# A scan kernel with experts: B as two float32r parts, and new lists of work

## What is computed

```python
delta = softplus(x @ Wd + bd)
Bm = x @ WB + bB                       # 16 values per token
Cm = x @ WC + bC
A = -exp(A_log)
def step(h, inps):
    x_t, d_t, B_t, C_t = inps
    bar_A = exp(minimum(d_t[:, :, None] * A, 2.0))
    bar_B = clip(d_t[:, :, None] * B_t[:, None, :], -2.0, 2.0)
    h = clip(bar_A * h + bar_B * x_t[:, :, None], -100.0, 100.0)
    return h, sum(h * C_t[:, None, :], -1) + x_t * D_param
routing = softmax(flat @ Wr + br)      # top 1 of 4 experts
hid = silu(flat @ up_w[e] + up_b[e])
out = ssm_out + top1_w * (hid @ down_w[e] + down_b[e])
x = layernorm(x + layernorm(out) * ln_w + ln_b)
x = layernorm(x + (silu(x @ wg.T) * (x @ wu.T)) @ wd.T)
```

## Time and profile before

| | us |
|---|---|
| runs: median of 3 (lowest, highest) | 859.77 (859.2, 875.19) |
| the profiled execution: its time | 854.52 |
| the profiled execution: its span | 852.7 |
| busy: DVE, PE, POOL, ACT | 706.2, 652.5, 558.3, 517.1 |
| a steady batch | 92.7 |
| after the last scan | 138.4 |

### The profile page before, as it was taken

One profiled execution on the slowest core, in us unless ns is written; L12 is line 12 of the kernel. 1 busy time (PEld: TensorE's weight loads), 2 busy tenths in 40 slices (PEclk: granted clock), 3 DMA queues, 4 the chain that ended last, 5 costly groups with the idle time before them and its releaser, 6 DMA issues.

```text
span 852.7 us, 14265 instructions
## 1 busy us (share of the span) xinstructions
PE 652.5 (77%) x4267; PEld 529.3 (62%) x4322; DVE 706.2 (83%) x1458; ACT 517.1 (61%) x970; POOL 558.3 (65%) x452
## 2 busy tenths in 40 slices
PE   3366567876789768995889778986988668889686
PEld 1144345864588547874688557964787447778555
DVE  3699999889999999799999999999979999324452
ACT  5274084777577946775777847784678413575534
POOL 1257458658875887578865886588766886525442
PEclk9587696997799959996799869995999859799988
DMA  3333346785467637674578536764667465375410
GB/s 110 123 127 121 127 146 208 244 265 163 146 221 241 204 118 229 201 214 169 171 236 249 177 120 223 237 210 154 209 190 228 140 198 185 107 219 181 132 37 26
DMA packets 82088, 149.32 MB, mean 175 GB/s; under 512 B 9404, under 2 KB 51144, under 8 KB 81992
## 3 DMA queue, kind: packets, MB, share of 16 engines
q1 hardware_dynamic: 69192, 135.13, 49.7%
q0 software_dynamic: 4096, 8.40, 3.1%
q10 hardware_dynamic: 8704, 4.72, 1.9%
HBM read 132.80 MB, written 15.40 MB: 174 GB/s over the span
## 4 chain that ended last, share of the span: by engine, by line
PE 32%; DVE 30%; issue 13%; POOL 12%; ACT 6%; DMA 5%; DVEq 1%; SPq 1%; another core or an unknown queue 0%; POOLq 0%; ACTq 0%
DVE state L1304 8%; DVE state L1318 7%; PE psU L767 6%; POOL prod L1350 5%; PE psT L781 5%; PE psY L637 4%; DVE psB L1299 4%; PE psD L661 3%; POOL rows_in L1371 3%; DMA xT_sb<-in_xT 2%; DMA weights<-in_w_pack 2%; DVE attn L1271 2%; PE psU L808 2%; PE psB L631 2%; PE psU L810 2%
## 5 line engine op out<-in xcount | busy, mean ns | idle before, releaser
L1350 POOL TENSOR_TENSOR prod<-state,c_wide 128x1024 f32<-128x1024 f32 x128 | 302.0, 2367 | 129.7 <-DVE state L1318 109.1
L1299 DVE TENSOR_TENSOR psB<-dx,psB 128x512 f32<-128x512 f32 x256 | 166.7, 684 | 19.3 <-PE psB L631 9.6
L631 PE MATMUL psB<-parts,sel 128*128 128x512 bf16 x202 | 94.0, 470 | 109.7 <-DVE state L1318 65.0
L893 ACT ACTIVATE decay<-delta,a_sb 128x1024 f32<-128x1024 f32 x128 | 141.4, 1141 | 50.1 <-DVE state L1318 48.8
L637 PE MATMUL psY<-ident,prod 128*128 128x128 f32 x1024 | 169.5, 323 | 2.6 <-DVE state L1318 1.5
L1318 DVE TENSOR_TENSOR_SCAN state<-decay,state,psB 128x512 f32<-128x512 f32 x128 | 163.3, 1276 | 8.7
L637 PEld LDWEIGHTS psY<-ident,prod 128*128 128x128 f32 x1024 | 152.0, 170 | 11.6 <-issue 7.9
L1304 DVE TENSOR_TENSOR_SCAN state<-decay,psB 128x512 f32<-128x512 f32 x128 | 155.2, 1213 | 0.1
L934 ACT ACTIVATE hid<-psU,weights 128x128 f32<-128x128 f32 x352 | 100.2, 370 | 50.1 <-PE psU L767 48.4
L631 PEld LDWEIGHTS psB<-parts,sel 128*128 128x128 bf16 x256 | 26.3, 103 | 160.7 <-DVE state L1318 92.7
L767 PE MATMUL psU<-yT_sorted,weights 128*128 128x128 f32 x704 | 95.8, 280 | 10.1 <-DMA weights<-in_w_pack 4.1
(11 more groups left out here) (163 smaller groups left out, 1030.0 us busy)
## 6 DMA issues: line engine op xcount, KB each, us to landing
c_wide<-c_rows SPq DMA_DIRECT2D x128, 512.0 KB, 5.0
weights<-in_w_pack SPq DMA_DIRECT2D x88, 514.0 KB, 4.0
xT_sb<-in_xT SPq DMA_DIRECT2D x8, 512.0 KB, 4.6
y_sorted<-rows_in SPq DMA_DIRECT2D x16, 256.0 KB, 3.3
xt<-in_x SPq DMA_DIRECT2D x8, 512.0 KB, 5.6
rows_out<-result SPq DMA_DIRECT2D x16, 256.0 KB, 5.3
out<-x ACTq DMA_DIRECT2D x16, 256.0 KB, 2.9
y_sorted<-rows_in SPq DMA_DIRECT2D x8, 192.0 KB, 4.8
```

Source lines behind the costliest of these rows:

```text
L631: pe.matmul(tokens(psB, c, h), sel[:, s, :], parts[:, c.n % 2, h * HALF:h * HALF + c.hw], start=True, stop=True).then_inc(b_ready, 1)
L893: nc.scalar.activation(decay[:, g % NDECAY, w], delta[:, n % 2, w], ACT.Exp, scale=a_sb[:, s:s + 1]).then_inc(decay_ready, 1)
L1299: v.tensor_tensor(tokens(psB, c, h), dx[:, n % 2, h * HALF:h * HALF + c.hw], tokens(psB, c, h), ALU.mult).then_inc(inp_ready, 1)
L1350: g_.tensor_tensor(prod[:, g % NPROD, w], state[:, g % NSTATE, w], c_wide[:, g % NC, w], ALU.mult).then_inc(prod_ready, 1)
```

## The change

B is cut in two float32r parts. `parts` and `sel` become float32r tiles; the matmul writes B and C to partitions 0 to 31 and 64 to 95 alone; ACT's second copy (`bc_mid`) works on 32 partitions and raises `parts_ready` itself; the DVE task `bc_low` goes, and so does the semaphore `parts_mid`. `sel` keeps one column per state, which the matmul reads 128 times. Beside that all the lists are new: the steady ones and those for the last batches. Line numbers behind L1123 fall by 4.

```diff
--- before.py
+++ after.py
 DVE_ORDER = [
...
-    (-2, "scan_rest", 10), (-1, "bc_low"), (-4, "affine", 1), (-4, "stats", 1, 1), (-4, "aggr", 1, 1),
+    (-2, "scan", 10), (-2, "scan_rest", 10), (-4, "centre", 1), (-4, "affine", 1), (-4, "stats", 1, 1),
...
@@ -365,7 +366,7 @@
         minus_ident = sb("minus_ident", [128, 128], F32R)
         ident127 = sb("ident127", [128, 128])
         selcol = sb("selcol", [128, S])
-        sel = sb("sel", [128, S, 128], BF16)
+        sel = sb("sel", [128, S], F32R)
         aux_sb = sb("aux_sb", [128, 129 + L // ROWS + MAX_BLOCKS])
         bias3 = sb("bias3", [96, D], BF16)
         of_block = sb("of_block", [96, 2, MAX_BLOCKS], BF16)
@@ -381,7 +382,7 @@
         zb = sb("zb", [D, L])
         sp = sb("sp", [D, L])
         bcf = sb("bcf", [128, L])
-        parts = sb("parts", [128, 2, L], BF16)
+        parts = sb("parts", [128, 2, L], F32R)
         bmax = sb("bmax", [128, 2 * NJ], BF16)
         delta = sb("delta", [D, 2, L])
         dx = sb("dx", [D, 2, L])
@@ -460,7 +461,6 @@
 
         parts_high = sem("parts_high")
         rest_ready = sem("rest_ready")
-        parts_mid = sem("parts_mid")
         parts_ready = sem("parts_ready")
         c_stored = sem("c_stored")
         softplus_steps = sem("softplus_steps")
@@ -628,7 +628,7 @@
                     pe.wait_ge(parts_ready, c.n + 1)
                     if c.n == 0:
                         pe.wait_ge(setup_dve, SETUP)
-                pe.matmul(tokens(psB, c, h), sel[:, s, :], parts[:, c.n % 2, h * HALF:h * HALF + c.hw],
+                pe.matmul(tokens(psB, c, h), sel[:, s:s + 1].to_broadcast([128, 128]), parts[:, c.n % 2, h * HALF:h * HALF + c.hw],
                           start=True, stop=True).then_inc(b_ready, 1)
 
             def add_turned(c, term, src, first, last, done):
@@ -668,7 +668,7 @@
                 pe.wait_ge(state_ready, S * (c.n + 1))
                 pe.wait_ge(gathered[0], 16 * NJ * (c.with_half[0] + 1))
                 for k in range(WARM):
-                    pe.matmul(psB[:, 0:HALF], sel[:, 0, :], parts[:, c.n % 2, 0:HALF], start=True, stop=True)
+                    pe.matmul(psB[:, 0:HALF], sel[:, 0:1].to_broadcast([128, 128]), parts[:, c.n % 2, 0:HALF], start=True, stop=True)
 
             def fill(b, c, task):
 
@@ -865,7 +865,7 @@
                     act.dma_start(c_rows[n % 2, :, w], bcf[S:2 * S, w]).then_inc(c_stored, 16)
                 if name == "bc_mid":
                     act.wait_ge(rest_ready, n + 1)
-                    nc.scalar.activation(parts[64:128, n % 2, w], rest[64:128, w], ACT.Copy).then_inc(parts_mid, 1)
+                    nc.scalar.activation(parts[64:96, n % 2, w], rest[64:96, w], ACT.Copy).then_inc(parts_ready, 1)
                 if name == "softplus":
                     exp_table()
                     wait(act, flag_steps, 2 * n - 1)
@@ -1028,7 +1028,7 @@
             v.memset(peak[:, :], 0.0).then_inc(consts_ready, 1)
             dve.wait_ge(consts_ready, 2)
             v.memset(first_block[:, 0:1], 0.0).then_inc(consts_ready, 1)
-            setup(v.tensor_copy(sel[:, :, :], selcol[:, :].rearrange("p (s o) -> p s o", o=1).to_broadcast([128, S, 128])))
+            setup(v.tensor_copy(sel[:, :], selcol[:, :]))
             setup(v.tensor_scalar(minus_ident[:, :], ident[:, :], -1.0, None, ALU.mult))
             setup(v.tensor_scalar(ident127[:, :], ident[:, :], 127.0, None, ALU.mult))
             dve.wait_ge(ff_in, 48)
@@ -1118,10 +1118,6 @@
                     dve.wait_ge(delta_ready, n + 1)
                     v.tensor_tensor(dx[:, n % 2, w], delta[:, n % 2, w], xT_sb[:, n % 2, w], ALU.mult
                                     ).then_inc(dx_ready, 1)
-                if name == "bc_low":
-                    dve.wait_ge(parts_mid, n + 1)
-                    v.tensor_tensor(parts[96:128, n % 2, w], rest[96:128, w], parts[96:128, n % 2, w], ALU.subtract
-                                    ).then_inc(parts_ready, 1)
                 if name == "bound":
                     (h,) = args
                     dve.wait_ge(delta_ready, n + 1)
@@ -1353,7 +1349,7 @@
                     pool.wait_ge(parts_high, n + 1)
 
                     wait(pool, flag_steps, 2 * n - 1)
-                    g_.tensor_tensor(rest[:, w], bcf[:, w], parts[:, n % 2, w], ALU.subtract).then_inc(rest_ready, 1)
+                    g_.tensor_tensor(rest[:, w], bcf[:, w], parts[:, n % 2, w].bitcast(F32), ALU.subtract).then_inc(rest_ready, 1)
                 if name == "bound_input":
                     pool.wait_ge(x_abs_ready, n + 1)
                     pool.wait_ge(dinv_ready, n + 1)
@@ -1425,7 +1421,7 @@
     pad = np.zeros(32, wb.dtype)
     bcb = np.concatenate([a["attn_bB"], a["attn_bC"]])
     sel = np.zeros((128, S), np.float32)
-    for row in (0, 64, 96):
+    for row in (0, 64):
         sel[row:row + S] = np.eye(S, dtype=np.float32)
     up_w, down_w = a["attn_up_w"], a["attn_down_w"]
     w_pack = np.concatenate([
@@ -1441,8 +1437,8 @@
     arrays = {
         "xT": x.transpose(0, 2, 1), "x": x, "a_log": a["attn_A_log"], "d_param": a["attn_D_param"].reshape(D, 1),
         "wd": a["attn_Wd"], "bd": a["attn_bd"].reshape(D, 1),
-        "wbc": np.concatenate([wb, wc, none, wb, wc, wb, wc], axis=1),
-        "bbc": np.concatenate([bcb, pad, bcb, bcb]).reshape(128, 1),
+        "wbc": np.concatenate([wb, wc, none, wb, wc, none], axis=1),
+        "bbc": np.concatenate([bcb, pad, bcb, pad]).reshape(128, 1),
         "wr": a["attn_Wr"], "br": a["attn_br"].reshape(1, E), "w_pack": w_pack,
         "biases": a["attn_down_b"], "aux": aux,
         "ln_w": a["attn_ln_w"].reshape(1, D),
```

262 lines of the change are left out of this document (133 added, 129 removed), and 3 rows, old and new, of the table SP_ORDER.

## The result

The changed kernel takes 880.0 us (median of 4 runs, 875.1 to 884.7), the kernel before 860.9 (median of 4, 859.2 to 875.2): ratio 1.022, 95% interval 1.016 to 1.028. It is slower by 2.2%, where 848 us and a small gain were forecast. The profiled execution took 877.7 us (span 875.9) against 854.5, at the same mean clock (0.851 of full speed in both).

The account below looks back on a forecast made before the run. No engine bounds alone; in steady batches DVE nearly does (88.0 of 92.7 us), PE next. First batch -1.0, two batches -2.5, five at -1.8 -9.0, tail +0.3: -12.2 us, 842.3 profiled, 848 as median, range 839 to 858.

Parts of the forecast that it names:

- the replay of `centre` 1 and `affine` 1 behind `scan_rest` 10: DVE, steady batch in new order: `centre` 1 stalls 1.12 us behind POOL's product 9, then all eight operations need 2.25 us.
- the 2.10 us stall: DVE's `affine` 1, slowed by POOL's L1361 (3.24 us against 1.14): claimed to go in five batches, -2.10 us each.
- -0.21 + 1.12 for `centre` 1: DVE, per steady batch: -0.21 us as `centre` 1 no longer waits for L1356, +1.12 us waiting behind product 9.
- the stall stays: Rival, chance 0.33: L1361 gets in front of one of the eight operations, DVE waits 2.1 us again; 855 us.
- The rival "Slower": Chance 0.08, 867 us: POOL comes first everywhere, so DVE's `centre` 1, `affine` 1 and `dx` wait 1.12, 2.10 and 2.36 us.
- its further part: Chance 0.02, 900 us: float32r matmul with one column read 128 times is slower than L808, +6.4 us a batch.
- The first batch's -1.0 us: First batch: dropped `bc_low` saves 1.3 us on the path, POOL's 4-byte subtraction costs 0.24; net about -1.0 us.
- the -2.5 us for the two steps without an `affine` 1: Two batches whose `bc_low` (76.7 and 152.9 us) has no `affine` 1 near: -1.26 us each, -2.5 in all.
- The float32r price: PE's spread matmuls: weight load 190 to 192 ns against 98, throughput unchanged; handovers +0.3 us per batch, tail +0.3.
- four direct places per batch: Handovers where `scan` s+1 directly follows `scan_rest` s (15-0, 1-2, 6-7, 11-12), eight before: each pays 0.1 us more at high clock.
- the dropped step's own time: DVE's `bc_low` (L1123), one instruction per batch, 8 in all: removing it frees 1.26 us each with the issue behind it.
- The steady batch of 90.5 to 91 us: Sign that the forecast is right: steady batch at 90.5 to 91 us, from 92.7, -1.8 us taken per batch.

Follow-up runs that it names:

- the mended one: The change with `centre` 1 back ahead of `scan_rest` 9, `combine` 0 ahead of `scan_rest` 3 (10 in last list), last list's first `combine` 1 ahead of `scan_rest` 15: 854.8 us.

## Why the prediction was wrong

**The step that failed** is the replay of `centre` 1 and `affine` 1 behind `scan_rest` 10: "So `centre` 1 stalls 1.12 us, until 427.07", then "With each piece at its length it ends at 429.3 to 429.5" for L868, and from both "So the 2.10 us stall goes". I replayed the batch with durations of another order and let the whole gain of -2.10 us hang on a margin of 0.1 us. Counted from the end of `scan_rest` 10, the replay had product 9 through at 1.1 us, the eight operations at 3.35 and the conversion at 3.35 to 3.55. In the five steady batches of the trace product 9 is through at 1.9 to 2.9 us and the conversion at 2.7 to 2.8, with the bound's input right behind it. Each of the two errors alone, the product later or the conversion sooner, closes the margin. The eight operations were to take 3.4 us and take 6.3 to 6.9. Against before, the forecast had -2.10 for `affine` 1 and -0.21 + 1.12 for `centre` 1, together -1.2 us; it was +1.4 to +2.3. In two batches `affine` 1 stayed as it was (within 0.1 us) and `centre` 1 took 1.4 and 1.8 us more. In the other three `affine` 1 did lose its stall, as forecast, and `centre` 1 took it over (4.3 to 4.4 us more).

**Slower than the rival "the stall stays".** That rival had this mechanism, at 855 us, with 3.2 us of stall for the two groups where 4.0 to 4.7 were measured, and allowed 0.3 us of gain per batch; the steady batches lost 3.1 us on average. Beside the longer stalls two things lie between. It held that a late `bound` 0 costs only the wait, but the wait also takes TensorE's clock more often: in four batches instead of two, at 1.4 to 1.6 us each between states 11 and 12. And it did not look at `combine` 0, moved by one entry across a `scan_rest`: 2.7 to 3.0 us in three batches of the trace, and in the timed runs 1.6% between the change and the kernel with it moved back (0.7% once `centre` 1 is back too). The diff showed the move; I checked only the neighbours of `bc_low`.

The rival "Slower", with a chance of 0.08 and 867 us, had the direction, but by `dx`, which came free; its further part, a slower load of one column read 128 times, did not come (190 ns). The first batch's -1.0 us was right (its first state ends 1.3 us earlier), but of the -2.5 us for the two steps without an `affine` 1 only one is to be seen: state 10 to 11 is 1.4 us shorter in the first batch and 1.3 us longer in the second, where `bound` 0 waits 1.21 us for the bound's input and the multiplications wait 0.82 and 0.95 us for the spread (with the old order and float32r parts it is 0.5 us shorter there).

**The float32r price was mis-sized.** The load was rightly read (98 to 190 ns, on the slow side), and also that throughput does not change and that a direct handover pays 0.1 us. The error was the count: four direct places per batch, +0.3 us per batch. (By the list before there are seven direct places and not eight.) Handovers with a short step between pay too, and so does the first batch, which is direct almost throughout. Measured: 1.1 to 1.7% in three orders (ratios 1.022 to 1.010, 1.000 to 0.982, 0.991 to 0.980), 9 to 15 us, where the sum held some 2. The pages bear out that most of it stands at the handovers: the multiplications and the idle time ahead of them sum to 187.7 us with bfloat16 parts and 196.3 with float32r in the new order, 185.9 and 195.9 in the old, 181.8 and 189.2 in the mended one, that is 7.4 to 10.0 us more. The cheaper subtraction of POOL, 0.25 us per batch, is in the rest.

**Right**: the dropped step's own time. Old order, two bfloat16 parts: -1.8%, 15 us, where the step by itself would account for 8 x 1.26 us = 10 us. Right too: POOL's subtraction (2.12 to 2.37 us, 0.24 predicted), ACT's conversion unchanged at 1.05 us, `dx` back at 1.20 us, and a tail within 1 us of before. The steady batch of 90.5 to 91 us was to be had as well: with `centre` 1 back PE no longer waits at that `down`, and the five batches take 90.4, 91.1, 91.5, 94.4 and 96.1 us, the last two with `combine` 0 stalled.

The kernel with `centre` 1 and both combines moved comes out at 854.8 us, 0.9% under the kernel before: what is left of the 2.0% that this order gives with two bfloat16 parts once the form is paid for.

What stays open: which of the other new entries make up the rest between orders. With two bfloat16 parts the old order (0.982) and the mended new one (0.980) are equal within their intervals; with float32r parts the mended one is 0.9% faster (0.991 against 1.000), and its multiplications with their waits take 189.2 us instead of 195.9. Why `combine` 0 is hit in some batches and runs and not in others is read from POOL's transfer issues and not tested by itself.
